# Moving the transposition of the quantized FFN weight behind the first attention outputs in an 8-core adaLN block on Trainium2

## What is computed

```python
mod = (silu(c) @ wmod)              # six vectors of 1024 for each batch element
sa, ca, ga, sb, cb, gb = ...        # |ga| and |gb| at least 0.25
h = layernorm(x) * (1 + ca) + sa
q, k = relu(h @ Wq.T) / 8, relu(h @ Wk.T) / 8
v, u = h @ Wv.T, silu(h @ Wu.T)
kv = einsum('bhlk,bhlv->bhkv', k, v)      # over all 2048 tokens
o  = einsum('bhlk,bhkv->bhlv', q, kv)
x  = x + ga * ((rms_normalized(o) * u) @ Wo.T)
h  = layernorm(x) * (1 + cb) + sb
w_q, w_scale = quantize_per_channel(weight)   # rounded to integers in +-127
x_q, x_scale = quantize_per_token(h)
x  = x + gb * ((x_q @ w_q.T) * x_scale * w_scale + bias)
```

## Time and profile before

| what | value |
|---|---|
| median of the two timed executions | 1269.47 us |
| the two of them | 1267.49 and 1271.45 us |
| the execution that was profiled, its own time | 1271.95 us |
| span of its slowest core (core 4), first to last instruction | 1269.5 us |
| spans of its eight cores | 1249.3 to 1269.5 us |
| busy share: TensorE, VectorE, ScalarE, GpSimd | 48%, 29%, 22%, 5% |
| mean granted TensorE clock of the cores | 0.714 to 0.722 of full speed |

### The profile page before, as it was taken

The page is one execution under the profiler, slowest core; times in us unless marked ns, Lnnn a source line. Parts: engine busy times, 40 slices in busy tenths (PEclk is TensorE's granted clock), DMA queues, the critical chain, the costliest instruction groups (busy, mean ns, idle before and its releaser), DMA issues.

```text
span 1269.5 us, 7729 instructions; the slowest of 8 cores (1249.3 to 1269.5 us)
## 1 busy us (share of the span) xinstructions
PE 606.0 (48%) x2344; PEld 236.4 (19%) x2344; DVE 373.6 (29%) x606; ACT 281.1 (22%) x418; POOL 65.0 (5%) x68
## 2 busy tenths in 40 slices
PE   0757657029869689990023620634125630436205
PEld 0101006004324234440010210201011210202102
DVE  0000000570050300001521464345541545424643
ACT  0000000033333242320443014311152012330142
POOL 0010000000000000000000000300003000200003
PEclk9988775559979889995555765757657665667657
DMA  8587660634020000007010000111002010020001
GB/s 198 138 187 188 204 149 1 100 66 67 1 34 1 1 1 1 1 1 198 0 33 1 18 16 0 67 33 33 1 1 100 0 34 0 0 100 28 6 0 66
DMA packets 33331, 65.68 MB, mean 52 GB/s; under 512 B 2437, under 2 KB 14854, under 8 KB 33294
## 3 DMA queue, kind: packets, MB, share of 16 engines
q0 software_dynamic: 17808, 44.04, 15.8%
q1 hardware_dynamic: 15486, 21.16, 5.0%
HBM read 75.69 MB, written 8.39 MB: 66 GB/s over the span
## 4 chain that ended last, share of the span: by engine, by line
PE 42%; DVE 22%; ACT 14%; DMA 13%; issue 7%; SPq 1%; DVEq 0%; ACTq 0%; POOLq 0%; POOL 0%; PEldq 0%
PE pb L67 42%; DMA wmq<-wmod 6%; DVE h L67 3%; DVE x_fma L67 3%; ACT o_bf L67 3%; DVE ouxq L67 2%; DVE M_sb L67 2%; DMA fwS<-ffn_w 2%; DVE x L67 2%; DVE xq_i L67 2%; DMA bias_c<-ffn_b 2%; DVE rowsB L67 2%; ACT h L67 2%; DMA x_fmb<-x_fm 2%; ACT L67 2%
## 5 line engine op out<-in xcount | busy, mean ns | idle before, releaser
L67 PE MATMUL pb<-wmq,silc 128*1 128x512 f32 x192 | 102.0, 693 | 88.4 <-DMA wmq<-wmod 50.4
L67 PE MATMUL pb<-ouxq,fqT 128*128 128x512 bf16 x256 | 64.3, 418 | 73.5 <-ACT ouxq L67 73.5
L67 PE MATMUL pb<-ouxq,woT 128*128 128x512 bf16 x256 | 66.8, 430 | 7.0 <-DVE ouxq L67 7.0
L67 DVE COPY mrow<-pb 1x512 f32<-1x512 f32 x12 | 8.1, 678 | 181.3 <-PE pb L67 181.3
L67 DVE TENSOR_REDUCE ws_c<-fwS 128x1 f32<-128x1024 f32 x8 | 9.1, 1210 | 156.6 <-DMA fwS<-ffn_w 156.6
L67 ACT ACTIVATE ouxq<-x 128x4096 bf16<-128x4096 f32 x4 | 14.5, 3617 | 175.3 <-DVE x L67 175.3
L67 DVE TENSOR_TENSOR h<-h,pb 128x512 f32<-128x512 f32 x64 | 41.3, 681 | 36.9 <-ACT o_bf L67 36.5
L67 ACT ACT_TABLE_LOAD x16 | 20.5, 1283 | 136.1 <-POOL amx L67 38.3
L67 PE MATMUL pb<-id_b,wqb 128*128 128x128 bf16 x64 | 9.4, 300 | 85.7 <-ACT wqb L67 55.5
L67 PE MATMUL pb<-h1a,wqT 128*128 128x512 bf16 x128 | 35.3, 445 | 29.3 <-ACT q_sb L67 29.3
L67 PEld LDWEIGHTS pb<-wmq,silc 128*1 128x1 f32 x192 | 17.1, 92 | 172.4 <-issue 172.4
(11 more groups left out here) (126 smaller groups left out, 1017.1 us busy)
## 6 DMA issues: line engine op xcount, KB each, us to landing
wmq<-wmod POOLq DMA_DIRECT2D x12, 2048.0 KB, 13.7
x_fmb<-x_fm SPq DMA_DIRECT2D x8, 1024.0 KB, 5.2
out_fm<-h SPq DMA_DIRECT2D x4, 2048.0 KB, 7.3
x_tm<-x_tm POOLq DMA_DIRECT2D x4, 1024.0 KB, 11.6
x_fma<-x_fm POOLq DMA_DIRECT2D x4, 1024.0 KB, 8.4
fwS<-ffn_w SPq DMA_DIRECT2D x1, 4096.0 KB, 26.0
wqT<-wq_t POOLq DMA_DIRECT2D x1, 2048.0 KB, 31.5
wkT<-wk_t POOLq DMA_DIRECT2D x1, 2048.0 KB, 23.9
```

The source lines that it names most:

```text
L67: ins = f(*a, **kw)
```

## The change

The order of emission is no longer the order of the code alone. Every recorded operation gets a number as its key, by default its place in the list; before emission the list is sorted by these keys, and the values that the semaphores must reach are counted along the sorted list. The 32 operations of the transposition get keys that put them behind the 24th operation of B0: behind the last `ssm`, before the copy of pb2 to rowsB. Nothing else gets a key of its own. The ten small constants that were given the semaphore value of the last of them get it now through an alias, which is the same value. Waits, tiles, banks and instructions are those of before.

```diff
+    def finalize(self):
+        self.sorted_ops = sorted(self.ops, key=lambda t: t[0])
+        counts = {}
+        self.evval = {}
+        for key, eng, emit, wn, inc, inc_n, n_ins, event in self.sorted_ops:
+            if inc is not None:
+                c = counts.get(inc.name, 0) + inc_n * max(n_ins, 1)
+                counts[inc.name] = c
+                if event is not None:
+                    self.evval[event] = (inc, c)
...
     def emit_engine(self, engine, eng):
-        for e, emit, wl, il, n_ins in self.ops:
+        if self.sorted_ops is None:
+            self.finalize()
+        for key, e, emit, wn, inc, inc_n, n_ins, event in self.sorted_ops:
             if e != engine:
                 continue
...
+            _tq_idxs.append(len(sch.ops))
             sch.op("tensor", tq(), waits=w, inc=sT, event=f"f_t{dcb}_{hf}")
...
+            _tq_idxs.append(len(sch.ops))
             sch.op("scalar", tqe(), waits=[f"f_t{dcb}_{hf}"], inc=sS,
                    event=f"f_te{dcb}_{hf}")
...
+    _P_B0 = float(len(sch.ops))
     for i in range(NT):
...
+    for _j, _oi in enumerate(_tq_idxs):
+        sch.ops[_oi][0] = _P_B0 + 23.5 + _j * 0.001
```

More of the change, by code:

```diff
@@ L78, in __init__, with op @@
         self.ops = []
-        self.events = {}
-        self.counts = {}
+        self.evset = set()
+        self.alias = {}
+        self.sorted_ops = None
     def sem(self, name):
[L83 to L88, removed]
+        return self.nc.alloc_semaphore(name)
+    def op(self, engine, emit, waits=(), inc=None, event=None, inc_n=1,
+           key=None):
+        for w in waits:
+            assert w in self.evset, f"unknown event {w}"
         mock = _CountEng()
@@ L91, in op, with alias_event @@
         n_ins = mock.n
[L92 to L102, removed]
+        if event is not None:
+            assert inc is not None
+            assert event not in self.evset, f"dup event {event}"
+            self.evset.add(event)
+        if key is None:
+            key = float(len(self.ops))
+        self.ops.append([key, engine, emit, tuple(waits), inc, inc_n,
+                         n_ins, event])
+    def alias_event(self, name, target):
+        assert target in self.evset and name in self.evset
+        self.alias[name] = target
+    def finalize(self):
[6 more added lines that the diff above has]
+                counts[inc.name] = c
+                if event is not None:
+                    self.evval[event] = (inc, c)
+        for name, target in self.alias.items():
+            self.evval[name] = self.evval[target]
     def emit_engine(self, engine, eng):
-        for e, emit, wl, il, n_ins in self.ops:
+        if self.sorted_ops is None:
+            self.finalize()
+        for key, e, emit, wn, inc, inc_n, n_ins, event in self.sorted_ops:
             if e != engine:
@@ L108, in emit_engine @@
             best = {}
-            for sem, v in wl:
+            for w in wn:
+                sem, v = self.evval[w]
                 if sem.name not in best or best[sem.name][1] < v:
@@ L113, in emit_engine @@
                 eng.wait_ge(sem, v)
-            if il and n_ins > 0:
-                sem, n = il[0]
-                prox = _IncEng(eng, sem, n)
+            if inc is not None and n_ins > 0:
+                prox = _IncEng(eng, inc, inc_n)
                 emit(prox)
@@ L120, in emit_engine @@
                 emit(eng)
-                for sem, n in il:
-                    eng.sem_inc(sem, n)
+                if inc is not None:
+                    eng.sem_inc(inc, inc_n)
 def build_nc():
@@ L273, in build_nc @@
     sch.op("sync", ld(bias_c[:], dfb.ap()), inc=sD, event="l_bias", inc_n=16)
-    _aux_total = sch.val(sD)
     for _ev in ("l_idb", "l_idf", "l_ones", "l_zcb", "l_mss", "l_mbc",
-                "l_sel", "l_selr", "l_c", "l_bias"):
-        sch.events[_ev] = (sD, _aux_total)
+                "l_sel", "l_selr", "l_c"):
+        sch.alias_event(_ev, "l_bias")
     NW = 12
@@ L674, in build_nc @@
         sch.op("scalar", wq2(), waits=[f"f_wqv{ec}"], inc=sS, event=f"f_wq{ec}")
+    _tq_idxs = []
     for dcb in range(NC):
```

## The result

The changed kernel took 1275.47 us in the median (28 executions), the kernel before 1270.83 us (27 executions, those of the prediction's two among them), so the medians lie 4.6 us apart. The ratio is 1.0048, with a 95% interval from 1.0033 to 1.0064. It compares means, 1275.9 and 1269.8 us, and leaves out two executions of each kernel that fell into a slower state, over 1.5% above its fastest. By it the change is slower by some 6 us (4 to 8), and far within the 2% that count as a difference. The prediction was 1273.1 us, +3.7 us or a ratio of 1.0029. Of the 2.4 us by which its time is too low, 1.4 us is its base: the two executions it started from had a median of 1269.47 us, the 27 have 1270.83 us.

A forecast was written before the change was run, and what follows sets the result against it. No single engine was taken as the bound, but a chain passing between engines. Seam terms 3.86 + 1.20 - 1.52 + 0.12 = +3.66 us on the 1269.47 us median gave 1273.1 us, range 1266 to 1280 us.

The forecast's parts named there:

- 1. first attention matmul: TensorE's first attention matmul, waiting for VectorE's 16 kv copies into kv_sb, comes 0.26 us after they end, at 648.27 us.
- 1. first o_bf: ScalarE's first attention output follows its matmul by 0.71 us, at 648.98 us; before, ScalarE's first ladder began at 645.12.
- 2. first o_bf to last sum: The eight attention rounds on TensorE and ScalarE, about 2.56 us each, keep their length of 19.26 us.
- 3. last sum to first copy: From attention rounds into transposition: 1.20 us newly on the path, while the 1.52 us wait before the table load goes.
- 4. 15 steps: The transposition, now behind the attention rounds, keeps its 15 steps of 1.515 us, 22.73 us.
- 4. last copy to table load: ScalarE's table load for the square root directly follows the transposition's last copy: 0.60 us after its start, 0.12 us more.
- Step 1, the lost cover: Start of attention: the kv copies (4.01 us), formerly hidden beside the transposition, now delay the first output, costing 3.86 us.
- Downstream: From the table load to the end, everything shifts by the full 3.66 us, with no slack to absorb it.
- Hidden ladders: Rival: transposition steps run in the attention rounds' gaps, table load 19.35 us early, 1250.1 us; chance 0.03.
- A warmer projection: Rival: TensorE's clock is already up when the output projection starts, worth 2.5 us, 1270.6 us; chance 0.07.
- Emptying before the table load: Rival: ScalarE must empty for 1.77 us before the square root's table load, +5.41 us, 1274.9 us; chance 0.06.
- Stretched steps: Rival: each moved transposition step takes 2.56 us in place of 1.515, +16.7 us, 1289.8 us; chance 0.02.

The follow-up runs named there:

- Experiment 6: Changed kernel with two transposition steps inside each of the eight attention rounds in place of all 16 behind them: 1252.12 us against 1268.41 us before, ratio 0.9875.

## Why the prediction was right

The mechanism was right at every step of the sum, and the sizes were too; the sum is best compared on core 4, counted from the last wqi.

| step | predicted | measured |
|---|---|---|
| 1. first attention matmul | 5.47 us behind | 647.00 - 641.64 = 5.36 us |
| 1. first o_bf | 6.18 us behind | 6.04 us |
| 2. first o_bf to last sum | 19.26 us | 666.94 - 647.68 = 19.26 us |
| 3. last sum to first copy | 1.20 us | 668.16 - 666.94 = 1.22 us |
| 4. 15 steps | 22.73 us | 691.01 - 668.16 = 22.85 us |
| 4. last copy to table load | 0.60 us | 0.61 us |
| whole distance | 49.97 us | 49.98 us |
| against before | +3.66 us | +3.67 us |

**Step 1, the lost cover.** Shown three ways: the bracket of 75.13 us names kv_sb, moving the copies took off 3.73 us, doubling them added 4.06 us, and neither did anything in the old order. The cost was taken a little high (0.14 us to the first o_bf). Most of it is the wait from the copies' end to the matmul, 647.00 - 646.85 = 0.15 us and not the 0.26 us of the earlier trace rows; the rest is 0.68 us in place of 0.71 us from there to the o_bf.

**Steps 2 to 4.** The rounds kept their length, and the first four matmuls lost their head start. The sums' copy ended at 668.38 us, under the first copy of the transposition; the prediction said the second step, but by its own times (669.7 against a first copy from 669.44) it was the first as well. The 15 steps took 0.12 us longer than before, since one of them has a wait of 1.08 us on both sides in place of 0.93 us (the row at 675.88). That the whole sum meets to 0.01 us is luck: -0.14 us in step 1 and +0.15 us behind it cancel.

**Downstream.** "Nothing downstream has slack to swallow it" fits these profiles, as far as a scatter of some 5 us between cores lets one see 3.7 us: the part from the projection to the end is 564.9 us before and 565.2 and 564.5 us in the two profiles of the changed kernel.

**The rivals.** Hidden ladders: excluded by the order, and priced at 19.35 us of gain over before. Experiment 6 made it true and gained 15.7 us of distance, 46.28 - 30.59. The price was too high because the rounds did not stay at 2.56 us with two steps inside; each grew to 3.04 us, and 8 x 0.48 = 3.8 us is about what is missing. A warmer projection: in the changed kernel too the clock stood at 0.50 throughout both ladders and the normalization, and for at least the first 5.3 us of the projection. The projection's run was 16.78 us against 16.70 us. One aside on the clock does not fit its rows: that ScalarE's two passes fill most of an attention round. They fill 1.09 us of 2.56 (647.68 to 648.77), and since the clock never rose there, no run tells what a round takes at the high level. Emptying before the table load: the gap is 691.62 - (691.01 + 0.58) = 0.03 us, so the rival is out. The Trainium skill ("ScalarE: Activation LUTs", "What ACT_TABLE_LOAD costs") would have put a drain of about 1380 ns there; this row and that of the earlier trace rows show none beside the load's 1.28 us. Stretched steps: 22.85 us for 15, not stretched.

**What did not come out as forecast.** The first measured ratio, 1.0048 (1.0033 to 1.0064), does not hold the predicted 1.0029; the second, 1.0029 (1.0005 to 1.0054), does. The two profiles of the changed kernel, 16 cores in all, show 3.67 us at the seam and, within the scatter of the other parts, no more elsewhere. Whether the remaining 2 us of the first measurement are scatter of the slowest core or something that the profiled executions did not have stays open. It changes no verdict: by both, the change is within 2%.

## What to carry to other kernels

Moving a block of operations past another, when both use the same two engines in turns, exchanged two ladders here and hid nothing; the gain is in putting the steps of one between those of the other (19.4 us here, with the same operations and the same waits). Before moving a block, look for what lies under it for free: here 4 us of copies that cost nothing as long as the transposition lay over them. And first look for a wait that is already there, since eight attention rounds and their copies cost nothing inside a 26 us load, and of the normalization only the 1.8 us of table load and square root stayed visible beside the transposition.

## What the runs showed of the hardware

The hand-over from ScalarE's square root to VectorE's clamp behind it was not constant. In the kernel before, the clamp started 691.49 - (690.40 + 0.63) = 0.46 us behind the end of ScalarE's square root; with the kv copies doubled in the same order it was 0.10 us, which is why the distance from table load to projection is 16.76 us there and 17.13 us before. The rows of that run, core 4:

```profile
680.60 1.28 ACT L67 ACT_TABLE_LOAD   x1 [1.76 <-DVE rowsB L67]
681.89 0.63 ACT L67 ACTIVATE rowsB<-rowsB 16x512 f32<-16x512 f32 x1
682.62 0.41 DVE L67 TENSOR_SCALAR rowsB<-rowsB 16x512 f32<-16x512 f32 x1 [2.10 <-ACT rowsB L67]
```

All eight cores of every run without doubled copies have 0.45 to 0.47 us; all eight of both runs with them have 0.10 to 0.11 us, and the changed order with doubled copies has the short distance too, 70.83 - 54.02 = 16.8 us on core 4. The doubled copies put 16 more instructions into VectorE's stream ahead of it and changed nothing else; why that shortens a wait by 0.36 us was not tried.
